# A perceiver kernel on one core: the first feed-forward tile is rounded before the second sequence's gates, and the second output product takes the place of filler matmuls

## The chip, the cores and the metric

One Trainium2 chip, one core. The metric is the device time of one execution in microseconds (us). Engines: PE (TensorE), DVE (VectorE), ACT (ScalarE), POOL (GpSimd) and SP, which here only issues DMAs. TensorE's clock has two levels, 1.2 and 2.4 GHz; the profile gives the granted one as a share of the higher.

## The reference

Two sequences of 256 tokens, 256 features, pass through two layers. What the change touches is the end of the gated mixer and the start of the quantised feed-forward block in layer 0, cut here to its lines:

```python
# gated mixer, end                       # L0_attn
y = _linear(y, fuse_w, fuse_b)
y = gate * y
y = _linear(y, out_w, out_b)
x = residual + y
# feed-forward                           # L0_ffn
h = layernorm(x, ln1_g, ln1_b)
h = bitlinear(h, w1, b1)                 # each row rounded to 8 bits, weights to -1, 0, 1
h = gelu(h)
h = layernorm(h, ln2_g, ln2_b)           # 1024 wide
h = bitlinear(h, w2, b2)
x = x + h
# next layer, cross-attention: scores of layernorm(x) with a context of 4096 rows
```

## The kernel before, in words

The kernel is one program per engine, written out by hand: each engine runs its instructions in the order in which the code lists them, and semaphores (`on[...]`, `wait_ge`, `then_inc`) join the engines. So the order of the lines is the schedule. The 512 tokens are four tiles of 128 rows (0 and 1 are the first sequence, 2 and 3 the second). The first sequence runs ahead: while the mixer of the second sequence is finished, tiles 0 and 1 already go through the feed-forward block.

On the DVE the steps here are `gate(1, m)` (L1505, four chunks of the second sequence, each out of one PSUM bank that `fuse(1, m)` on PE filled), `hidden(0, n)` (L1567: two halves of 512 columns for each tile, PSUM to UH), `hidden_stats` (L1574), `aggregate` (L1429), `ask_root` (L1415, which asks POOL for a power of the variance), `gain` (L1587), `take_power` (waits for POOL), `shift` (L1597), `find_scale` (L1540 to L1546), `quantise_hidden` (L1606 to L1611, which counts up `d_quant2`). After that a tile goes to PE: `turn_hidden(i)` (eight bf16 transposes, L2279), then ACT's `copy_hidden(i)` (L1057), then `project_down(i)` (L2213, eight bf16 matmuls), then DVE's `add_down` (L1614 and statistics) and `centre_for_keys` (L1450), and PE's `turn_tile` (L2292), `queries_tile` and `fold_tile` (L2200, eight fp32 matmul instructions each) and at last the `key_scores` of the next layer (L2448), whose first unit stands behind `turn_hidden(1)` in PE's order.

`project_out(1)` (L2213, 16 instructions) is the mixer's output product of the second sequence. It needs all eight gates; its result is added to X by `add_mixed(2, 4)` (L1510) on DVE. `keep_awake(bank, n)` (L2112) issues n bf16 matmuls of 512 columns whose result nobody reads; they fill PE's waits. ACT's `gelus` (L1048) follow `hidden`. POOL's `power` (L767) computes the roots in the order in which they are asked for.

SP loads the next layer's mask and context (L611); before the first of them it waits for `c_out` at 4, that is the end of `project_out(1)`, and for `d_turned2` at 1, that is `turn_hidden(0)`:

```python
            sp.wait_ge(on["c_out"], 4)
            sp.wait_ge(on["d_turned2"], 1)
```

Of the kernel before, what the change touches and what calls it, by code (L numbers as in the profile page):

```python
# [19 lines left out]
TT = T // P  # L20
# [21 lines left out]
IT = DI // P  # L42
# [107 lines left out]
def build(nc, t):  # L150

    ctx = ExitStack()
    with ctx:
# [3 lines left out]
        def sem(name):  # L157
            return ctx.enter_context(nc.semaphore(name))
# [119 lines left out]
        OUT_BANKS = (7, 0, 3, 4)  # L278
        QUANT_BANK = (1, 3)
        UP_BANKS = ((7, 0, 2, 1), (7, 3, 7, 3))  # L280
        DOWN_BANKS = (5, 6, 3, 7)
        QUERY_BANKS = ((0, 1), (3, 4), (7, 3))
        QC_BANKS = (2, 5, (7, 3))
        CQ_BANK = (5, 6, 7)
# [1 line left out]
        def tile(i):  # L286
            return slice(i * P, (i + 1) * P)

        def batch(b):
            return slice(b * S, (b + 1) * S)  # L290
# [153 lines left out]
        on = {name: sem(name) for name in SIGNALS}  # L444
# [242 lines left out]
        def _(pool):  # L687
# [74 lines left out]
            def power(first, last):  # L762

                powers[0] += 1
                pool.wait_ge(ln_var, powers[0])
                part = SD[:, 4 + first:4 + last]
                nc.gpsimd.tensor_tensor(part, part, NHALF[:, first:last], ALU.pow).then_inc(ln_sd, 1)  # L767

            power(0, 1)
            power(1, 2)  # L770
            power(0, 1)
            power(1, 2)
            power(0, 1)
            power(2, 4)
            power(1, 2)
            power(2, 4)
# [25 lines left out]
        def _(act):  # L802
# [155 lines left out]
            def signal(ins, name):  # L958
                ins.then_inc(on[name], 1)
# [73 lines left out]
            def copy_quantised_tile(i):  # L1033
                act.wait_ge(on["d_turned"], i + 1)
                signal(nc.scalar.activation(HQT[:, :, tile(i)],
                                            psum[:, QUANT_BANK[0], 0:256].bitcast(BF16)
                                            .rearrange("p (c n) -> p c n", c=CT)[:, :, tile(i)], ACT.Copy), "d_turned_copied")
# [6 lines left out]
            def gelus(first, last):  # L1044
                for n in range(first, last):
                    act.wait_ge(on["d_hidden"], n + 1)
                    part = UH[n // 2][:, 0, n % 2 * 512:(n % 2 + 1) * 512]
                    signal(nc.scalar.activation(part, part, ACT.Gelu), "d_gelu")  # L1048
# [6 lines left out]
            def copy_hidden(i):  # L1055
                act.wait_ge(on["d_turned2"], i + 1)
                signal(nc.scalar.activation(QHT[i].rearrange("p k n -> p (k n)"),  # L1057
                                            psum[:, DOWN_BANKS[i], :].bitcast(BF16), ACT.Copy), "d_turned2_copied")

# [6 lines left out]
            def copy_turned_tile(i):  # L1066
                act.wait_ge(ht_psum, CT * (turns[0] + 1))
                nc.scalar.activation(HTE[:, :, tile(i)], psum[:, 7, :].rearrange("p (c n) -> p c n", c=CT)[:, :, tile(i)],
                                     ACT.Copy).then_inc(ht_ready, CT)
                turns[0] += 1  # L1070
# [38 lines left out]
            copy_quantised_tile(0)  # L1109
            gelus(0, 2)  # L1110
            copy_quantised_tile(1)
            gelus(2, 4)
            copy_hidden(0)
            copy_turned_tile(0)
            copy_queries_tile(0)
            copy_folded_tile(0)
# [115 lines left out]
        def _(dve):  # L1232
# [90 lines left out]
            def mark(ins):  # L1323

                ins.then_inc(on["step_v"], 1)
                steps[0] += 1

            def done():

                dve.wait_ge(on["step_v"], steps[0])  # L1330
# [94 lines left out]
            def aggregate(n, first=0, last=TT):  # L1425

                done()
                for i in range(first, last):
                    mark(nc.vector.bn_aggr(MV[:, 2 * i:2 * i + 2], BN[:, 12 * i:12 * i + 6 * n]))  # L1429
                done()  # L1430
# [72 lines left out]
            def gate(b, m):  # L1503
                dve.wait_ge(on["c_fuse"], IT * b + m + 1)
                nc.vector.scalar_tensor_tensor(out=YG[:, m, batch(b)], in0=psum[:, FUSE_BANKS[b][m], 0:S],  # L1505
                                               scalar=col("fuse_b", m), in1=GATE[:, m, batch(b)],
                                               op0=ALU.add, op1=ALU.mult).then_inc(on["c_gated"], 1)
# [56 lines left out]
            def hidden(b, n):  # L1564
                i, at = 2 * b + n // 2, slice(n % 2 * 512, (n % 2 + 1) * 512)
                dve.wait_ge(on["d_up"], 4 * b + n + 1)
                nc.vector.scalar_tensor_tensor(out=UH[i][:, 0, at], in0=psum[:, UP_BANKS[b][n], :],  # L1567
                                               scalar=OSC[:, i:i + 1], in1=row("w1b")[:, at],
                                               op0=ALU.mult, op1=ALU.add).then_inc(on["d_hidden"], 1)

            def hidden_stats(b, n):
                i = 2 * b + n // 2
                dve.wait_ge(on["d_gelu"], 4 * b + n + 1)
                mark(nc.vector.bn_stats(BN[:, 12 * i + n % 2 * 6:12 * i + n % 2 * 6 + 6],  # L1574
                                        UH[i][:, 0, n % 2 * 512:(n % 2 + 1) * 512]))

            def add_down_bias(*tiles):
                done()
                for i in tiles:
                    mark(nc.vector.tensor_tensor(X[:, i, :], X[:, i, :], row("w2b"), ALU.add))  # L1580
# [24 lines left out]
            def quantise_hidden(i):  # L1605
                mark(nc.vector.tensor_scalar(UH[i][:, 0, :], UH[i][:, 0, :], QSC[:, i:i + 1], ROUND,  # L1606
                                             ALU.mult, ALU.add))
                done()
                mark(nc.vector.tensor_scalar(QH[i], UH[i][:, 0, :], ROUND, 127.0, ALU.subtract, ALU.min))
                done()  # L1610
                nc.vector.tensor_scalar(QH[i], QH[i], -128.0, None, ALU.max).then_inc(on["d_quant2"], 1)  # L1611

            def add_down(first, last, ahead):
                add_to_x("d_down", 2, lambda i: nc.vector.scalar_tensor_tensor(  # L1614
                    out=X[:, i, :], in0=psum[:, DOWN_BANKS[i], 0:256], scalar=OSC[:, i:i + 1], in1=X[:, i, :],
                    op0=ALU.mult, op1=ALU.add), first, last, ahead)
                ask_root(first, last)

            def centre_for_keys(*tiles):
                take_power()  # L1620
                for i in tiles:
                    centred(HLE, X, i).then_inc(h_ready, 1)
# [13 lines left out]
            hidden(0, 0)  # L1636
            hidden(0, 1)
            gate(1, 0)
            gate(1, 1)
            hidden_stats(0, 0)  # L1640
            hidden_stats(0, 1)
            aggregate(2, 0, 1)
            ask_root(0, 1)
            gate(1, 2)
            hidden(0, 2)
            hidden(0, 3)
            gain(0)
            gate(1, 3)
            take_power()
            shift(0)  # L1650
            find_scale(0)
            quantise_hidden(0)
            hidden_stats(0, 2)
            hidden_stats(0, 3)
            aggregate(2, 1, 2)
            ask_root(1, 2)
            add_down_bias(0, 1)
            gain(1)
            take_power()
            done()  # L1660
            add_down(0, 1, TT + 2)
            shift(1)
            centre_for_keys(0)
            find_scale(1)
            quantise_hidden(1)
            add_mixed(2, 4, TT + 3)
# [283 lines left out]
        def _(pe):  # L1950
# [158 lines left out]
            def keep_awake(bank, n):  # L2109

                for _ in range(n):
                    nc.tensor.matmul(psum[:, bank, :], IDENTB, IDENTB.unsqueeze(1).broadcast_to((P, 4, P)),  # L2112
                                     start=True, stop=True)
# [140 lines left out]
            def project_out(b):  # L2254
                pe.wait_ge(on["c_gated"], IT * (b + 1))
                for i in (2 * b, 2 * b + 1):
                    linear_rows(psum[:, OUT_BANKS[i], 0:256], tok(YG, i), WOUT, False, "c_out")
# [18 lines left out]
            def turn_hidden(i):  # L2276
                pe.wait_ge(on["d_quant2"], i + 1)
                for k in range(FT):
                    last = nc.tensor.transpose(psum[:, DOWN_BANKS[i], k * 64:(k + 1) * 64].bitcast(BF16),  # L2279
                                               QH[i][:, k * P:(k + 1) * P], IDENTB)  # L2280
                last.then_inc(on["d_turned2"], 1)

            def project_down(i):
                pe.wait_ge(on["d_turned2_copied"], i + 1)
                linear_rows(psum[:, DOWN_BANKS[i], 0:256], [QHT[i][:, k, :] for k in range(FT)], TW2, False, "d_down")

# [40 lines left out]
            def mix():  # L2327
# [83 lines left out]
                project_up(0, 2)  # L2411
                project_up(0, 3)
                fuse(1, 3)
                project_out(1)
                keep_awake(6, 8)

            any_masked = pe.value_load(FLAG, min_val=0, max_val=1)
            with pe.If(any_masked == 0):
# [3 lines left out]
            with pe.Else():  # L2422
                attend(True)
                mix()

            pe.wait_ge(on["d_hidden"], 4)
            turn_hidden(0)
            keep_awake(2, 4)
            project_down(0)
            keep_awake(2, 12)  # L2430
            pe.wait_ge(on["l1w_loaded"], 64)
            turn_tile(HLE, 0, 2 * TT)
            keep_awake(2, 2)
# [456 lines left out]
```

## Time and profile before

| | |
|---|---|
| median of 3 runs | 899.23 us (899.07 to 899.90) |
| the profiled execution, whole | 899.97 us |
| its span | 898.2 us |
| mean granted TensorE clock | 0.998 |
| PE busy | 870.7 us (97%) |
| DVE busy | 606.6 us (68%) |
| ACT busy | 479.8 us (53%) |
| POOL busy | 141.4 us (16%) |

The profiled execution took 1.77 us outside its span and stands 0.74 us above the median. All times of rows are counted from the span's start. Matmul ends are modelled, so a matmul can seem to begin a little before the one ahead of it has ended. In PE's rows an fp32 matmul is two instructions, while the listing of the program's order counts it once.

### The profile page before, as it was taken

The page shows a single profiled execution, that of the slowest core. Times are in us where ns is not written, and L with a number is a line of the kernel's source. Part 1 is how long each engine was busy: PE and PEld are TensorE (multiplying, and loading weights), DVE is VectorE, ACT ScalarE, POOL GpSimd, SP SyncE. Part 2 cuts the span into 40 slices and gives each one's busy share as a digit, 9 for nine tenths or more (in the row PEclk, how much of TensorE's full clock was granted, in tenths as well). Part 3 has the DMA queues.
Part 4 walks back from the last instruction along what each step waited for, and adds up shares of the span by engine and source line. Part 5 has one row for each costly group of instructions (what it writes and reads, how often), then busy time and mean ns, then how long its engine had stood idle before and what let it go on. Part 6 is the DMA issues. An engine that isn't in the chain of part 4 may idle for free.

```text
span 898.2 us, 15321 instructions
## 1 busy us (share of the span) xinstructions
PE 870.7 (97%) x6029; PEld 518.3 (58%) x6031; DVE 606.6 (68%) x1060; ACT 479.8 (53%) x973; POOL 141.4 (16%) x144
## 2 busy tenths in 40 slices
PE   8899999999999999999999999999999999999998
PEld 4556444444556665555545587654884784656745
DVE  6988877778885556888872589977724228379352
ACT  5452666777775566777779852214411310668221
POOL 7353111111000000000000260010100006345100
PEclk9999999999999999999999999999999999999999
DMA  9989564453523112222613440084645705000000
GB/s 353 301 262 221 132 169 113 118 165 112 129 66 90 36 36 72 72 71 72 191 37 136 169 178 1 1 292 138 227 188 186 282 22 167 1 1 1 1 1 24
DMA packets 55083, 108.50 MB, mean 121 GB/s; under 512 B 5409, under 2 KB 38177, under 8 KB 49825
## 3 DMA queue, kind: packets, MB, share of 16 engines
q1 hardware_dynamic: 52832, 103.29, 37.5%
q10 hardware_dynamic: 2176, 4.19, 1.7%
q8 instruction: 50, 0.82, 0.4%
q14 instruction: 25, 0.20, 0.1%
HBM read 93.58 MB, written 13.89 MB: 120 GB/s over the span
## 4 chain that ended last, share of the span: by engine, by line
PE 82%; DVE 11%; ACT 2%; DMA 2%; issue 1%; POOL 1%; SPq 0%; DVEq 0%; ACTq 0%
PE psum L2049 14%; PE psum L2031 13%; PE psum L1998 11%; PE psum L2448 6%; PE psum L2476 6%; PE psum L1961 5%; PE psum L2580 5%; PE psum L1971 4%; DVE arena L1528 3%; PE psum L2213 3%; PE psum L2645 2%; PE psum L2630 2%; PE psum L2200 2%; DVE arena L1281 1%; PE psum L2669 1%
## 5 line engine op out<-in xcount | busy, mean ns | idle before, releaser
L1281 DVE TENSOR_REDUCE arena<-psum 128x1 f32<-128x1024 f32 x256 | 300.9, 1218 | 97.3 <-PE psum L1998 96.8
L849 ACT ACTIVATE arena<-psum 128x512 f32<-128x512 f32 x512 | 263.1, 602 | 67.0 <-PE psum L2031 65.9
L1998 PE MATMUL psum<-arena 120*128 120x512 bf16 x512 | 151.7, 379 | 5.7 <-DVE arena L1281 3.4
L2031 PE MATMUL psum<-arena 120*128 120x256 bf16 x1024 | 154.8, 274 | 1.8 <-ACT arena L849 0.5
L2049 PE MATMUL psum<-arena 128*32 128x256 f32 x2048 | 137.0, 385 | 0.0
L2031 PEld LDWEIGHTS psum<-arena 120*128 120x128 bf16 x1024 | 80.5, 97 | 96.2 <-ACT arena L849 36.7
L2049 PEld LDWEIGHTS psum<-arena 128*32 128x32 f32 x2048 | 53.4, 109 | 74.2 <-ACT arena L849 30.7
L711 POOL TENSOR_TENSOR arena<-arena 128x512 bf16<-128x512 f32 x34 | 41.4, 1219 | 158.3 <-DVE arena L1267 140.4
L1971 PE MATMUL psum<-arena 128*128 128x256 f32 x256 | 63.2, 384 | 0.0
L1998 PEld LDWEIGHTS psum<-arena 120*128 120x128 bf16 x512 | 48.7, 98 | 23.4 <-DVE arena L1281 11.9
L1961 PE MATMUL psum<-arena 128*128 128x512 f32 x128 | 60.9, 603 | 0.0
L2476 PE MATMUL psum<-arena 128*128 128x256 f32 x256 | 57.9, 379 | 0.0
L2448 PE MATMUL psum<-arena 128*128 128x512 f32 x128 | 57.2, 595 | 0.0
L1971 PEld LDWEIGHTS psum<-arena 128*128 128x128 f32 x256 | 47.7, 191 | 13.1 <-issue 5.3
L2476 PEld LDWEIGHTS psum<-arena 128*128 128x128 f32 x256 | 47.5, 190 | 5.8
L735 POOL MEMSET arena<- 128x32 f32 x1 | 0.1, 129 | 288.9 <-PE psum L2049 288.9
L2200 PE MATMUL psum<-arena 128*128 128x256 f32 (+1 forms) x208 | 44.2, 366 | 0.4 <-ACT arena L1075 0.2
L821 ACT ACTIVATE arena<-psum,arena 128x512 bf16<-128x512 f32 x32 | 22.0, 689 | 39.2 <-PE psum L1961 35.6
L832 ACT ACTIVATE arena<-psum 128x512 f32<-128x512 f32 x32 | 19.1, 597 | 44.4 <-PE psum L1971 44.4
L2580 PE MATMUL psum<-arena 128*128 128x512 f32 x96 | 42.8, 596 | 0.0
L2200 PEld LDWEIGHTS psum<-arena 128*128 128x128 f32 x208 | 37.1, 190 | 7.5 <-issue 1.4
L2448 PEld LDWEIGHTS psum<-arena 128*128 128x128 f32 x128 | 23.7, 190 | 25.7 <-issue 24.9
(269 smaller groups left out, 1024.3 us busy)
## 6 DMA issues: line engine op xcount, KB each, us to landing
arena<-mask SPq DMA_DIRECT2D x12, 1024.0 KB, 6.1
kparts<-arena SPq DMA_DIRECT2D x32, 384.0 KB, 3.4
arena<-kparts SPq DMA_DIRECT2D x32, 384.0 KB, 4.6
arena<-ctxT SPq DMA_DIRECT2D x16, 512.0 KB, 5.9
arena<-kparts SPq DMA_DIRECT2D x32, 256.0 KB, 5.1
arena<-ctx SPq DMA_DIRECT2D x2, 4096.0 KB, 17.3
arena<-ctxT ACTq DMA_DIRECT2D x8, 512.0 KB, 8.2
arena<-kparts SPq DMA_DIRECT2D x32, 128.0 KB, 5.5
```

Of the source, the lines that this page charges most:

```text
L711: nc.gpsimd.tensor_tensor(parts[:, 2, :], rest, parts[:, 1, :], ALU.subtract).then_inc(k_low, 1)
L849: nc.scalar.activation(PR[step % 4][:, pair * CH:(pair + 1) * CH], exp_bank(step, pair), ACT.Exp, scale=DH ** -0.5)\
L1281: nc.vector.tensor_reduce(MX[g % 2][:, col:col + 1], unit_banks(n).rearrange("p b n -> p (b n)"), AX.X, ALU.max).then_inc(s_maxed, 1)
L1961: last = nc.tensor.matmul(ring_bank(slot), WK[:, k, f * P:(f + 1) * P], CTX[n % SLOTS][:, k, :], start=(k == 0), stop=(k == CT - 1))
L1971: last = nc.tensor.matmul(ring_bank(slot)[:, v * 256:(v + 1) * 256], CTX[n % SLOTS][:, k, (2 * i + v) * P:(2 * i + v + 1) * P], WV[:, k, : ...
L1998: last = nc.tensor.matmul(out, q, KST[g % 2][0:ROWS, quarter, j, half * CH:(half + 1) * CH], start=True, stop=not masked, skip_group_check ...
L2031: last = nc.tensor.matmul(heads[:, u, :], KST[gg % 2][0:ROWS, kc // 8, j, kc % 8 * P:(kc % 8 + 1) * P], QST[0:ROWS, b, G * g + j, :], star ...
L2049: last = nc.tensor.matmul(PV[32 * j:32 * (j + 1), :], V_flat[:, at:at + 32], PR[step % 4][:, j * S:(j + 1) * S], start=(kc == 0), stop=(kc ...
L2200: last = nc.tensor.matmul(out, weights[:, k, m * P:m * P + width], xs[k], start=(k == 0), stop=(k == n - 1))
L2448: last = nc.tensor.matmul(psum[:, unit % 3, :], QC[:, c, w * P:(w + 1) * P], CTXT[w // 2][:, c, n * 512:(n + 1) * 512], start=(c == 0), st ...
L2476: last = nc.tensor.matmul(psum[:, 6, 0:256], PT1[:, k * P:(k + 1) * P], CTXK[w // 2][:, k, :], start=(k == 0), stop=(k == KC - 1), skip_gr ...
L2580: last = nc.tensor.matmul(out, HTF[:, c, i * P:(i + 1) * P], WQKV[which][:, c, half * HALF:(half + 1) * HALF], start=(c == 0), stop=(c == ...
```

## The change

On DVE everything of tile 0 up to its rounding now stands directly behind its two `hidden` halves and `gate(1, 0)`. The three other gates, tile 1's two `hidden` halves and all of tile 1's steps come behind it. The bias rows and `add_down` of tile 0 stand ahead of tile 1's statistics. On PE `project_out(1)` and the fillers ahead of the branch's end go; `turn_hidden(0)` and `project_down(0)` come first, with 12 and 5 fillers ahead of and between them, and `project_out(1)` stands where 12 fillers stood. Of the four places with 8, 4, 12 fillers (24 in all), 17 are left. Tile 0's transposes and its down product use PSUM bank 0 in place of bank 5. ACT copies tile 0's transposes ahead of tile 1's gelus. On POOL the two requests change places to match.

```diff
-        DOWN_BANKS = (5, 6, 3, 7)
+        DOWN_BANKS = (0, 6, 3, 7)
...
             power(0, 1)
             power(1, 2)
             power(0, 1)
+            power(0, 1)
             power(1, 2)
-            power(0, 1)
...
             copy_quantised_tile(1)
+            copy_hidden(0)
             gelus(2, 4)
-            copy_hidden(0)
...
             gate(1, 0)
-            gate(1, 1)
             hidden_stats(0, 0)
             hidden_stats(0, 1)
             aggregate(2, 0, 1)
             ask_root(0, 1)
-            gate(1, 2)
-            hidden(0, 2)
-            hidden(0, 3)
             gain(0)
-            gate(1, 3)
             take_power()
             shift(0)
             find_scale(0)
             quantise_hidden(0)
+            for m in range(1, IT):
+                gate(1, m)
+            hidden(0, 2)
+            hidden(0, 3)
+            add_down_bias(0, 1)
+            done()
+            add_down(0, 1, TT + 2)
             hidden_stats(0, 2)
             hidden_stats(0, 3)
+            centre_for_keys(0)
             aggregate(2, 1, 2)
             ask_root(1, 2)
-            add_down_bias(0, 1)
             gain(1)
             take_power()
-            done()
-            add_down(0, 1, TT + 2)
             shift(1)
-            centre_for_keys(0)
             find_scale(1)
             quantise_hidden(1)
...
                 fuse(1, 3)
-                project_out(1)
-                keep_awake(6, 8)
...
+            pe.wait_ge(on["d_hidden"], 1)
+            keep_awake(7, 12)
+            turn_hidden(0)
+            keep_awake(7, 5)
+            project_down(0)
             pe.wait_ge(on["d_hidden"], 4)
-            turn_hidden(0)
-            keep_awake(2, 4)
-            project_down(0)
-            keep_awake(2, 12)
+            project_out(1)
             pe.wait_ge(on["l1w_loaded"], 64)
             turn_tile(HLE, 0, 2 * TT)
```

DVE's order behind tile 0's first statistics, as a piece of the difference (the names are those given above; L1505 is a gate, L1567 a hidden half, L1587 the gain, L1597 the shift):

```order
 L1574 BN_STATS arena<-arena 128x6 x2
 L1429 BN_AGGR arena<-arena 128x2
 L1415 TENSOR_SCALAR arena<-arena 128x1
-L1505 SCALAR_TENSOR_TENSOR arena<-psum,arena 128x256
-L1567 SCALAR_TENSOR_TENSOR arena<-psum,arena 128x512 x2
 L1587 SCALAR_TENSOR_TENSOR arena<-arena 128x1024
-L1505 SCALAR_TENSOR_TENSOR arena<-psum,arena 128x256
 L1597 SCALAR_TENSOR_TENSOR arena<-arena 128x1024
 L1540 TENSOR_REDUCE arena<-arena 128x1
```

The request to POOL (L1415) is now followed at once by the gain, and the gain at once by the shift; a gate and two hidden halves stood between the first two and a gate between the others.

The next piece, from the end of tile 0's rounding up to tile 1's shift:

```order
+L1574 BN_STATS arena<-arena 128x6 x2
+L1450 TENSOR_SCALAR arena<-arena 128x256
+L1429 BN_AGGR arena<-arena 128x2
+L1415 TENSOR_SCALAR arena<-arena 128x1
+L1587 SCALAR_TENSOR_TENSOR arena<-arena 128x1024
 L1597 SCALAR_TENSOR_TENSOR arena<-arena 128x1024
-L1450 TENSOR_SCALAR arena<-arena 128x256
 L1540 TENSOR_REDUCE arena<-arena 128x1
```

Tile 1's statistics, its request, gain and shift now stand in a row, behind tile 0's centring (L1450), which stood between tile 1's shift and its scale.

PE before, from `project_out(1)` to the first key scores:

```order
3019 L2213 MATMUL psum<-arena 128x256 x8
3020 L2112 MATMUL psum<-arena 128x512 x8
3021 L2422 UNCONDITIONAL_BRANCH
3022 L2279 MATMUL psum<-arena 128x128 x8
3023 L2112 MATMUL psum<-arena 128x512 x4
3024 L2213 MATMUL psum<-arena 128x256 x8
3025 L2112 MATMUL psum<-arena 128x512 x12
3026 L2292 MATMUL psum<-arena 128x128 x2
3027 L2112 MATMUL psum<-arena 128x512 x2
3030 L2200 MATMUL psum<-arena 128x128 x4
3031 L2279 MATMUL psum<-arena 128x128 x8
3032 L2448 MATMUL psum<-arena 128x512 x2
```

PE now, in the same place (line numbers are one lower than before):

```order
3017 L2419 UNCONDITIONAL_BRANCH
3018 L2111 MATMUL psum<-arena 128x512 x12
3019 L2278 MATMUL psum<-arena 128x128 x8
3020 L2111 MATMUL psum<-arena 128x512 x5
3021 L2212 MATMUL psum<-arena 128x256 x16
3022 L2291 MATMUL psum<-arena 128x128 x2
3023 L2111 MATMUL psum<-arena 128x512 x2
3026 L2199 MATMUL psum<-arena 128x128 x4
3027 L2278 MATMUL psum<-arena 128x128 x8
3028 L2447 MATMUL psum<-arena 128x512 x2
```

The row of 16 is `project_down(0)` with `project_out(1)` behind it; from the turned tile (L2292, now L2291) on the two orders are the same, and the last transposes (L2278) are tile 1's.

## Rows read from the trace of the kernel before

**Rows 1.** The page: the chain that ended last, its shares of the span by engine.

```profile
PE 82%; DVE 11%; ACT 2%; DMA 2%; issue 1%; POOL 1%; SPq 0%; DVEq 0%; ACTq 0%
```

**Rows 2.** Chain that ended last, 587 to 597 us: start us, us, what.

```profile
587.00 1.53 POOL arena L767
...
596.60 5.15 PE psum L2448 x12
```

**Rows 3.** Timeline of DVE: start us, us, engine, line, op, count [idle before <-releaser].

```profile
569.36 1.40 DVE L1567 SCALAR_TENSOR_TENSOR arena<-psum,arena 128x512 f32<-128x512 f32 x2
...
571.43 0.48 DVE L1505 SCALAR_TENSOR_TENSOR arena<-psum,arena 128x256 f32<-128x256 f32 x1 [0.27 <-PE psum L2200]
571.83 1.28 DVE L1574 BATCH_NORM_STATS2 arena<-arena 128x6 f32<-128x512 f32 x2
...
576.88 1.28 DVE L1597 SCALAR_TENSOR_TENSOR arena<-arena 128x1024 f32<-128x1024 f32 x1
...
581.46 0.43 DVE L1611 TENSOR_SCALAR arena<-arena 128x1024 bf16<-128x1024 bf16 x1
...
585.58 0.48 DVE L1614 SCALAR_TENSOR_TENSOR arena<-psum,arena 128x256 f32<-128x256 f32 x1 [0.20 <-DVE arena L1587]
...
586.84 1.27 DVE L1597 SCALAR_TENSOR_TENSOR arena<-arena 128x1024 f32<-128x1024 f32 x1
588.63 0.41 DVE L1450 TENSOR_SCALAR arena<-arena 128x256 f32<-128x256 f32 x1 [0.52 <-POOL arena L767]
...
592.22 0.43 DVE L1611 TENSOR_SCALAR arena<-arena 128x1024 bf16<-128x1024 bf16 x1
...
595.52 0.69 DVE L1676 CUSTOM_DVE_ANT_0 arena<-psum,arena 128x512 f32<-128x512 f32 x1 [1.06 <-PE psum L2448]
```

**Rows 4.** Timeline of POOL: three of its powers.

```profile
563.84 0.73 POOL L767 TENSOR_TENSOR arena<-arena 128x1 f32<-128x1 f32 x1 [1.07 <-DVE arena L1417]
573.62 0.55 POOL L767 TENSOR_TENSOR arena<-arena 128x1 f32<-128x1 f32 x1 [9.05 <-DVE arena L1415]
...
587.00 1.52 POOL L767 TENSOR_TENSOR arena<-arena 128x1 f32<-128x1 f32 x1 [2.76 <-DVE arena L1415]
```

**Rows 5.** Timeline of DVE beside the first of these powers.

```profile
563.68 0.48 DVE L1551 SCALAR_TENSOR_TENSOR arena<-arena 128x256 f32<-128x256 f32 x1
```

**Rows 6.** Timeline of PE, 577 to 594 us.

```profile
577.02 3.72 PE L2213 MATMUL psum<-arena 128*128 128x256 f32 x16 [1.14 <-DVE arena L1505]
580.58 1.89 PE L2112 MATMUL psum<-arena 128*128 128x512 bf16 x8
582.30 0.61 PE L2279 MATMUL psum<-arena 128*128 128x128 bf16 x8
...
584.03 1.05 PE L2213 MATMUL psum<-arena 128*128 128x256 bf16 x8 [0.25 <-ACT arena L1057]
...
589.19 0.41 PE L2292 MATMUL psum<-arena 128*128 128x128 f32 x2 [1.53 <-DVE arena L1450]
...
592.75 0.61 PE L2279 MATMUL psum<-arena 128*128 128x128 bf16 x8
```

**Rows 7.** Timeline of PE, 32 us: the longest wait ahead of a fall of the clock.

```profile
32.59 0.39 PE L2152 MATMUL psum<-arena 128*128 128x8 f32 x2 [2.30 <-DVE arena L1274]
```

**Rows 8.** Busy time by stretch: stretch, us, PE, PEld, DVE, ACT, POOL busy (x), PEclk, DMA share, GB/s.

```profile
33.00:34.00 1.00, 1.00 (x5) 0.90 (x5) 0.93 (x5) 0.00 (x0) 0.33 (x1) 0.90 0.93 213
34.00:35.00 1.00, 1.00 (x3) 0.77 (x3) 1.00 (x1) 0.00 (x0) 0.83 (x1) 0.50 0.92 213
...
37.00:38.00 1.00, 1.00 (x3) 0.22 (x1) 0.73 (x1) 0.00 (x0) 0.64 (x2) 0.89 0.99 221
...
588.00:590.00 2.00, 0.81 (x4) 0.36 (x4) 1.49 (x3) 0.30 (x1) 0.53 (x1) 1.00 0.94 390
```

**Rows 9.** Timeline of the DMA queue of SP: issues of the mask, and their landing.

```profile
583.00 0.82 SPq L611 DMA_DIRECT2D arena<-mask  x2
...
arena<-mask SPq DMA_DIRECT2D x4, 1024.0 KB, 5.0
```

## The prediction

> **What bounds the kernel now.** I read the page's chain first: 82% of the span lies on PE and 11% on DVE [rows 1]. So a microsecond counts where PE waits, or where DVE holds it. Then I read the chain between 557 and 597 us, where the change lies. Up to 593 us it runs mostly over DVE, with one wait for a POOL power [rows 2]; from the first key scores on it stays on PE without a gap (12 instructions in 5.15 us) [rows 2]. The timelines of DVE and PE show why. Two things meet at tile 1's transposes, `turn_hidden(1)` (592.75 us) [rows 6]: PE comes from `fold_tile(0)` just then, and DVE's last rounding instruction of tile 1 ends at 592.22 + 0.43 = 592.65 us [rows 3]. PE is not early: it had been held until 589.19 us by tile 0's centring, with a wait of 1.53 us [rows 6]. The reader should take from this that PE and DVE reach this point together. Whatever happens before it is worth time only if both come earlier, since the key scores stand behind these transposes in PE's order.
>
> **Tile 0 on DVE.** Between `hidden(0, 1)` and the first shift the change takes out three gates and two hidden halves. A gate takes 0.40 us from start to start (571.43 to 571.83), three 1.20, and a wait of 0.27 goes with the first [rows 3]. The two halves are one entry of 1.40 us, 1.32 without the overlap to the next [rows 3]. That is 2.79 us, with small gaps 2.87. Against it stands a new wait. The request to POOL is now followed at once by the gain, an instruction with two SBUF operands of 1024 columns. The trace has that arrangement once, with a shift in place of the gain: the shift began at 586.84 and took 1.27; the power, begun at 587.00, took 1.52 and ended at 588.52, and DVE went on at 588.63 after an idle of 0.52 [rows 3, 4]. With a PSUM operand beside it a power took 0.55 [rows 4]. A third power, begun at 563.84 inside an SBUF pair that ran from 563.68 for 0.48, took 0.73 [rows 4, 5]. In both blocked cases POOL ended 0.41 us after DVE's instruction did. So from gain to shift it is 588.63 - 586.84 = 1.79 us, where 1.31 (1.27 and a drain) would do: the wait costs 0.48. Tile 0's rounding, which ended at 581.46 + 0.43 = 581.89 [rows 3], comes 2.87 - 0.48 = 2.39 earlier, at 579.50.
>
> The Trainium skill says the same of the mechanism (page "SBUF — State Buffer", section "SBUF: two separate sides"): VectorE and GpSimd share a port pair that is locked for a whole instruction, also by a VectorE operation with two SBUF inputs, and the later one waits. The trace agrees, with 1.52 against 0.55 us [rows 4]. [...]
>
> **Tile 1 on DVE, the end that counts.** Up to tile 1's rounding DVE runs the same instructions in both kernels, so only its idle time decides. Before, there were three waits: 0.27 for PE, 0.20 ahead of `add_down`, 0.52 for POOL, 0.99 in all [rows 3]. Now two remain, each a power behind which a gain runs at once: 2 x 0.48 = 0.96. So the rounding of tile 1 ends at 592.65 - 0.99 + 0.96 = 592.62, and with 0.15 from end to release (588.63 + 0.41 to 589.19 [rows 3, 6]) PE begins its transposes at 592.8, where it began at 592.75. **This part is worth 0.0 us**, between -1.0 (no power is held up) and +0.4 (drains between instructions that now stand in another order).
>
> **PE.** `fuse(1, 3)` ended at 577.02 - 1.14 = 575.88 [rows 6]. Twelve fillers at 1.89 / 8 = 0.24 [rows 6] last until 578.7; PE waits for tile 0's rounding until 579.65. From these transposes to the down product it was 584.03 - 582.30 = 1.73 [rows 6], ACT's copy included; so the down product starts at 581.4 and ends at 582.4. `project_out(1)` takes 3.72 [rows 6] and ends at about 586.0. DVE meanwhile: 579.5 and three gates 1.2, two halves 1.4, the bias rows 0.8 (an estimate, two instructions of a gate's width), `add_down` with its statistics 586.84 - 585.58 = 1.26, tile 1's statistics 1.28, centring 0.41 [rows 3], that is 585.8. Both are ready at about 586.0, where it was 589.19. The queries and their folding took until 592.75, 3.56 us, and now end at 589.5. The gain of 3.2 us stops there: **PE waits from 589.5 to 592.8, 3.3 us**, without a filler. The 24 - 17 = 7 fillers that go (1.6 us) lay in waits and are worth nothing on the path.
>
> **The clock.** The longest wait of PE in the trace in the middle of work is 2.30 us, ahead of 32.59 us [rows 7]. 1.2 us after its end the granted clock fell from 2.4 to 1.2 GHz: the five stretches of 1 us from 33 to 38 have 0.90, 0.50, 0.50, 0.50, 0.89 (three of them are [rows 8], the two left out have 0.50 too), in all 1.71 us lost. The wait of 1.53 us behind fillers did not do it: the stretch 588 to 590, with PE busy 0.81 of 2 us, has 1.00 [rows 6, 8]. The new wait of 3.3 us lies above both, and in the 3.5 us before it PE has short waits as well. I expect the fall. What it costs: PE pays only while it works. If the fall comes as long after the last matmul as it did there (30.3 to 33.8 us), it comes at 593.0 and all of the 1.7 us is paid by the key scores, which nothing hides. If it comes inside the wait, a part goes by unused; halfway in, 0.85. Nearest to the row is the full price, but the moment need not repeat; I take 1.5.
>
> **Transfers.** The masks wait for both `project_out(1)` and `turn_hidden(0)`. They were issued at 583.00 [rows 9]; now `project_out(1)` is the later, so 586.0. With 5.0 us to landing [rows 9] they are there at 591, and the first mask is read at 595.52 [rows 3]: nothing, with 4.5 us in hand. Bank 0 was last read by `hidden(0, 1)`, at 570.7: nothing. ACT is idle where its copy moves to: nothing. If ACT still had tile 1's gelus ahead, the copy would come 1.3 us later; they now stand behind it and wait for DVE anyway.
>
> **Sum.** 899.97 (own time of the profiled execution) + 0.0 + 1.5 = 901.5; against the median, which is 0.74 lower, 899.23 + 1.5 = **900.7 us**.
>
> **Rivals.** (a) The clock stays at 2.4 GHz: 899.2. For it speaks that all waits below 2.3 us went by without a fall; against it the 3.3 us. (b) The powers are not held up, by shorter locks or since POOL gets in first: DVE is 0.96 earlier, 898.3 with a steady clock, 899.8 with a fall. Against it speak two held-up powers out of two. (c) The gain of 3.2 us on PE is kept: 896.0. It would need tile 1's rounding at 589.5, and DVE has no 3 us of idle to give up (0.99). (d) Slower: the low clock is not left after one stretch like that of rows 8. While PE stands partly idle in the stretch after the fall, it may stay down for a second one, 2 x 1.7 = 3.4 us: 902.6. It decides if the fall comes well inside the wait, since then the next stretch holds waiting as well. (e) The change is not what it says on PE, if the fillers ahead of the transposes held up tile 0: they end at 578.7, 0.9 us early, so no.
>
> **Chances.** A measurement tells 0.2% (1.8 us, 897.4 and 901.0) from no change. Forecast, one fall: 0.68, of which about 0.22 comes out above 901.0 by a full price and drains of 0.1 to 0.4. (a) 0.13. (b) 0.06. (c) 0.03. (d) 0.10. So faster 0.04, same 0.63, slower 0.33. The range takes in (a) and most of (b) with a fall, and most of (d): 898.9 to 902.3.
>
> **What would show it.** PE waits over 3 us ahead of the second L2278 and DVE's L1611 ends within 0.4 us of 592.65; both powers of this place take 1.5 us. Tile 0's turned tile (L2291) starts at 586. A stretch with a granted clock of 0.5 lies between 591 and 597 us; key scores of 1.72 us last twice as long in it. Wrong would be: a clock of 1.00 throughout, L1611 a microsecond early, or a wait of the first mask for its DMA.

## The result, and the profile after

The changed kernel takes 901.15 us in the median of 22 runs (899.92 to 903.34); the kernel before, run beside it, 899.83 us in 22 runs. The ratio of the two is 1.0018 with a 95% interval of 1.0012 to 1.0024: slower by 1.3 us, an amount just under the 0.2% that the prediction took as the border of "same". The forecast was +1.5 us and 900.7 us.

DVE first. The timeline of DVE in the changed kernel: start us, us, engine, line, op, forms, count [idle before <-releaser]. This execution reached `hidden(0, 0)` at 570.02 where the one before had 569.36 [rows 3], so 0.66 us are to be taken off to compare.

```profile
570.02 1.40 DVE L1567 SCALAR_TENSOR_TENSOR arena<-psum,arena 128x512 f32<-128x512 f32 x2
...
573.36 1.27 DVE L1587 SCALAR_TENSOR_TENSOR arena<-arena 128x1024 f32<-128x1024 f32 x1
575.15 1.28 DVE L1597 SCALAR_TENSOR_TENSOR arena<-arena 128x1024 f32<-128x1024 f32 x1 [0.51 <-POOL arena L767]
...
579.73 0.43 DVE L1611 TENSOR_SCALAR arena<-arena 128x1024 bf16<-128x1024 bf16 x1
...
583.36 0.48 DVE L1614 SCALAR_TENSOR_TENSOR arena<-psum,arena 128x256 f32<-128x256 f32 x1
...
586.44 1.28 DVE L1587 SCALAR_TENSOR_TENSOR arena<-arena 128x1024 f32<-128x1024 f32 x1
588.23 1.28 DVE L1597 SCALAR_TENSOR_TENSOR arena<-arena 128x1024 f32<-128x1024 f32 x1 [0.51 <-POOL arena L767]
...
592.82 0.43 DVE L1611 TENSOR_SCALAR arena<-arena 128x1024 bf16<-128x1024 bf16 x1
...
598.00 0.69 DVE L1675 CUSTOM_DVE_ANT_0 arena<-psum,arena 128x512 f32<-128x512 f32 x1 [2.95 <-PE psum L2447]
```

Tile 0's rounding (first L1611) ends at 580.16, less the offset 579.50, where it ended at 581.89: 2.4 us earlier. Tile 1's (second L1611) ends at 593.25, less the offset 592.59, where it ended at 592.65: the same. The waits of 0.27, 0.20 and 0.52 us [rows 3] have gone, and two of 0.51 us for POOL have come: idle time on DVE is about what it was.

POOL in the changed kernel, its timeline at the same place:

```profile
573.52 1.52 POOL L767 TENSOR_TENSOR arena<-arena 128x1 f32<-128x1 f32 x1 [8.29 <-DVE arena L1415]
584.78 0.55 POOL L767 TENSOR_TENSOR arena<-arena 128x1 f32<-128x1 f32 x1 [9.74 <-DVE arena L1415]
586.60 1.52 POOL L767 TENSOR_TENSOR arena<-arena 128x1 f32<-128x1 f32 x1 [1.27 <-DVE arena L1415]
```

The first and third power run beside a gain, the second beside statistics, which read one SBUF operand. Of three equal operations two take 1.52 us and one 0.55.

PE in the changed kernel, its timeline from the down product on:

```profile
580.22 0.62 PE L2278 MATMUL psum<-arena 128*128 128x128 bf16 x8 [1.09 <-DVE arena L1611]
...
581.95 4.50 PE L2212 MATMUL psum<-arena 128*128 128x256 bf16 x24
586.36 0.41 PE L2291 MATMUL psum<-arena 128*128 128x128 f32 x2
...
588.92 1.16 PE L2199 MATMUL psum<-arena 128*128 128x128 f32 x8 [0.24 <-ACT arena L1075]
593.30 1.03 PE L2278 MATMUL psum<-arena 128*128 128x128 bf16 x8 [3.22 <-DVE arena L1611]
594.12 3.73 PE L2447 MATMUL psum<-arena 128*128 128x512 f32 x4
```

Tile 0's turned tile starts at 586.36 (585.70 less the offset), where it started at 589.19 [rows 6]: 3.5 us earlier. All of it ends up in one wait of 3.22 us ahead of tile 1's transposes. The unit of key scores behind it then takes 3.73 us. The busy time in stretches of 1 us shows why (stretch, us, PE, PEld, DVE, ACT, POOL busy (x), PEclk, DMA share, GB/s):

```profile
591.00:592.00 1.00, 0.00 (x0) 0.00 (x0) 0.96 (x3) 0.00 (x0) 0.00 (x0) 1.00 0.99 418
592.00:593.00 1.00, 0.00 (x0) 0.00 (x0) 0.93 (x3) 0.00 (x0) 0.00 (x0) 0.50 0.97 410
...
597.00:598.00 1.00, 1.00 (x4) 0.48 (x3) 0.00 (x0) 0.00 (x0) 0.00 (x0) 0.50 1.13 356
598.00:599.00 1.00, 1.00 (x7) 0.86 (x7) 0.70 (x2) 0.00 (x0) 0.00 (x0) 0.58 1.06 344
```

The granted clock fell from 2.4 to 1.2 GHz at 592.0, 1.3 us before PE had work again, and stayed there to 598.8. The 12 instructions of key scores that follow began at 596.60 [rows 2], 27.24 us after `hidden(0, 0)`; now the chain of work that ended last (start us, us, what) has them at 599.60, 29.58 us after it, so this execution paid 2.3 us:

```profile
593.30 1.03 PE psum L2278 x8
594.33 3.52 PE psum L2447 x4
597.85 0.65 PE psum L2306 x4
598.50 1.11 PE psum L2212 x8
599.60 5.15 PE psum L2447 x12
```

The other executions have no trace, but each has a mean granted clock: 15 of 22 have 0.996, four less, one 0.998 and two 1.00. Those two took 899.92 and 900.00 us. In the 35 executions of the kernel before that ran with the first experiments, 24 have 0.998, ten 1.00 and one 0.996.
The masks were issued later, as expected, and no instruction waited for them; the first masked score waited for PE (2.95 us above). The DMA queue of SP:

```profile
586.49 0.82 SPq L611 DMA_DIRECT2D arena<-mask  x2
```

### The profile page after: what moved, and what is told of

Its sections match the earlier page's. It is cut to its first block, busy times and chain, and to the rows that moved or that the text cites. A ratio compares the mean times of both kernels' runs of the same rounds, so it can differ in the third digit from the quotient of the medians.

```text
span 901.2 us, 15308 instructions
## 1 busy us (share of the span) xinstructions
PE 870.7 (97%) x6024; PEld 519.2 (58%) x6024; DVE 607.0 (67%) x1060; ACT 480.0 (53%) x973; POOL 142.3 (16%) x144
## 4 chain that ended last, share of the span: by engine, by line
PE 82%; DVE 12%; ACT 2%; issue 2%; DMA 1%; POOL 1%; SPq 0%; DVEq 0%; ACTq 0%
PE psum L2048 14%; PE psum L2030 13%; PE psum L1997 12%; PE psum L2447 6%; PE psum L2475 6%; PE psum L1970 5%; PE psum L2579 5%; PE psum L1960 5%; DVE arena L1528 3%; PE psum L2212 3%; DVE arena L1281 2%; PE psum L2644 2%; PE psum L2629 2%; PE psum L2668 1%; PE psum L2459 1%
## 5 line engine op out<-in xcount | busy, mean ns | idle before, releaser
L1970 PEld LDWEIGHTS psum<-arena 128*128 128x128 f32 x256 | 48.0, 192 | 13.4 <-issue 5.9
L2475 PEld LDWEIGHTS psum<-arena 128*128 128x128 f32 x256 | 47.5, 190 | 5.8
L2199 PEld LDWEIGHTS psum<-arena 128*128 128x128 f32 x208 | 37.1, 190 | 7.5 <-issue 1.4
L1675 DVE CUSTOM_DVE_ANT_0 arena<-psum,arena 128x512 f32<-128x512 f32 x32 | 22.0, 691 | 25.6 <-PE psum L2447 23.2
```

Of the source, the lines that this page charges most:

```text
L1970: last = nc.tensor.matmul(ring_bank(slot)[:, v * 256:(v + 1) * 256], CTX[n % SLOTS][:, k, (2 * i + v) * P:(2 * i + v + 1) * P], WV[:, k, : ...
L2199: last = nc.tensor.matmul(out, weights[:, k, m * P:m * P + width], xs[k], start=(k == 0), stop=(k == n - 1))
L2475: last = nc.tensor.matmul(psum[:, 6, 0:256], PT1[:, k * P:(k + 1) * P], CTXK[w // 2][:, k, :], start=(k == 0), stop=(k == KC - 1), skip_gr ...
```

## The experiments

All ratios are to the kernel before, run beside each group. The first question was whether the clock is all of the loss.

**Fillers in the wait.**

```diff
             fold_tile(0)
+            keep_awake(6, 13)
             turn_hidden(1)
```

> The changed kernel with 13 fillers (2.8 us) between fold_tile(0) and turn_hidden(1), where PE waited 3.22 us. DVE and everything else are as changed. Theory A (the loss is the fall of TensorE's clock in that wait): the granted clock stays at 1.00 from 586 to 600 us, tile 1's rounding still ends when it did after the change, the key scores take 1.72 us a unit from the first on, and the time goes back to that of the kernel before, 899.8 us, 1.3 us under the changed kernel. Theory B (the loss is something else that came with the change, a later end of DVE, the later masks or the order of the output product): the clock is back but the time stays at 901.1 us.

Measured: 899.75 us against 899.89, ratio 0.9995 (0.9986 to 1.0004). The executions' mean clock is 0.998 in nine and 1.00 in two of 11. PE's timeline of this kernel:

```profile
589.52 2.97 PE L2111 MATMUL psum<-arena 128*128 128x512 bf16 x13
592.89 0.62 PE L2278 MATMUL psum<-arena 128*128 128x128 bf16 x8 [0.41 <-DVE arena L1611]
593.35 1.94 PE L2448 MATMUL psum<-arena 128*128 128x512 f32 x4
```

Theory A holds. Thirteen matmuls that compute nothing take the loss away, and what the rest of the change costs or gains lies within the interval, -1.3 to +0.4 us.

**The reverse, on the kernel before.**

```diff
             project_down(0)
-            keep_awake(2, 12)
```

> The kernel before without the 12 fillers behind project_down(0); nothing else differs. PE then waits 4.2 us in place of 1.5 for tile 0's centring at 589 us. Theory A (a wait of that length drops the clock and the drop costs time): the granted clock falls to 0.5 between 587 and 592 us, the queries and the folding, and perhaps the first key scores, run at half speed, and the time rises by 0.5 to 1.7 us to 900.3 to 901.5 us, with DVE's rounding of tile 1 still at 592.65 us. Theory B (fillers and the clock do not matter here): 899.8 us, clock 1.00.

Measured: 901.36 us against 899.89, ratio 1.0016 (1.0008 to 1.0025), and a mean clock of 0.996 or less in ten of 11 executions. PE's timeline, and one stretch of busy time (columns as above):

```profile
589.81 0.66 PE L2292 MATMUL psum<-arena 128*128 128x128 f32 x2 [4.12 <-DVE arena L1450]
...
595.11 0.61 PE L2279 MATMUL psum<-arena 128*128 128x128 bf16 x8
```

```profile
588.00:590.00 2.00, 0.19 (x1) 0.23 (x2) 1.48 (x3) 0.00 (x0) 1.14 (x1) 0.50 1.00 422
```

With the wait at 4.12 us the clock is at 1.2 GHz before PE goes on. The queries and their folding, 3.56 us before, take 595.11 - 589.81 = 5.30 us, so tile 1's transposes come 1.7 us later, although DVE's rounding is where it was (the offset of this execution, 0.62 us, taken off). In this trace the clock is low once only, in one piece from 588.0 to 594.8 us, and the mean is 0.996: the same mean as two separate falls would give. Theory A again: a loss of the same size, with nothing of the change in the kernel.

**Half the fillers.** As the first edit, with `keep_awake(6, 6)`.

> The changed kernel with 6 fillers in place of 13 ahead of turn_hidden(1), so that 1.8 us of PE's wait are left. Theory A (it is the length of the wait that drops the clock; in the kernel before 1.5 us of wait did not): the mean clock is that of the kernel before (0.998) in nearly all executions, 899.8 us. Theory B (any wait here drops it, since PE was only partly busy ahead of it): a mean clock of 0.996 in most executions, 900.5 to 901 us.

Measured: 900.61 us against 900.16, ratio 1.0007 (0.9998 to 1.0016); the mean clock is 0.996 in seven of 11 executions, 0.998 in two, 1.00 in two. The execution with the profile is one of the last kind, so its trace shows the wait but no fall:

```profile
588.96 1.46 PE L2111 MATMUL psum<-arena 128*128 128x512 bf16 x6
592.34 0.62 PE L2278 MATMUL psum<-arena 128*128 128x128 bf16 x8 [1.92 <-DVE arena L1611]
```

By the executions' mean clock theory A fails here: with a wait of about 1.9 us at this place most executions have a low stretch more than usual, though with 1.53 us the kernel before did not (34 of 35). The time, 0.45 us above the kernel before, does not decide it, since its interval takes in no change. The two waits differ in more than 0.4 us. The one of 1.53 stood behind 12 fillers in a row; this one behind six, ahead of which PE had waited 0.24 us for a copy of ACT. Which of the two matters, the length or the work ahead, was not separated.

**Real work in the wait.** The first unit of key scores goes ahead of tile 1's transposes.

```diff
             fold_tile(0)
-            turn_hidden(1)
             pe.wait_ge(on["e_qc_copied"], 1)
...
             key_scores(0, 0)
+            turn_hidden(1)
             bias_tile(0)
             project_down(1)
```

> The changed kernel with the first unit of key scores, key_scores(0, 0), ahead of turn_hidden(1) on PE, so that real work lies in the wait. Theory A (PE's 3.2 us were gained and stop at tile 1's transposes): the unit runs at full clock from about 590.6 to 592.4 us, the wait for tile 1's rounding falls to about 0.6 us, the clock stays at 1.00, and the end comes 1.7 us earlier than with a steady clock alone: 898.1 us, 3 us under the changed kernel. Theory B (DVE sets the stretch after it too, since the masked scores wait behind tile 1's rounding and the adding of the mixer): the clock is steady but nothing else is gained, 899.8 us.

Measured: 899.02 us against 899.89, ratio 0.9993 (0.9984 to 1.0001). PE's timeline, the last row being tile 1's turned tile behind the next key scores:

```profile
589.53 1.99 PE L2445 MATMUL psum<-arena 128*128 128x512 f32 x4 [0.47 <-ACT arena L1080]
592.27 0.62 PE L2278 MATMUL psum<-arena 128*128 128x128 bf16 x8 [0.76 <-DVE arena L1611]
...
594.01 1.05 PE L2212 MATMUL psum<-arena 128*128 128x256 bf16 x8 [0.72 <-ACT arena L1057]
...
600.05 0.38 PE L2291 MATMUL psum<-arena 128*128 128x128 f32 x2
```

The same row in the kernel before:

```profile
601.59 0.38 PE L2292 MATMUL psum<-arena 128*128 128x128 f32 x2
```

The gain came out between the theories: the median is 0.9 us under the kernel before in place of 1.7, but by its interval the time alone does not tell it from no change. The trace does. Up to tile 1's turned tile the same work has been done in both; it starts 601.59 - 569.36 = 32.23 us after `hidden(0, 0)` before, and 600.05 - 569.00 = 31.05 us after it here, 1.2 us less. The trace also names what is missing: the moved unit had covered ACT's copy of tile 1 (L1057), and without it PE waits 0.72 us ahead of the down product. My expectation had left that cover out. The next run puts another unit there.

```diff
             key_scores(0, 0)
             turn_hidden(1)
+            key_scores(0, 1)
             bias_tile(0)
             project_down(1)
-            key_scores(0, 1)
             key_scores(0, 2)
```

> As the run with key_scores(0, 0) ahead of turn_hidden(1), but with key_scores(0, 1) moved between turn_hidden(1) and project_down(1). There PE had waited 0.72 us for ACT's copy of tile 1, which the moved unit had covered. Theory A (1.7 us of work moved, 0.7 given back by that uncovered copy): the wait of 0.72 us goes, the masked scores on DVE follow their unit as before, and the time falls by 0.5 to 0.7 us more, to 898.4 us. Theory B (DVE's masked scores, released later than their units, bound this stretch): the wait comes back ahead of key_scores(0, 3), which needs the first bank, and the time stays at 899.0 us.

Measured: 897.90 us against 900.16, ratio 0.9975 (0.9966 to 0.9984).

```profile
593.72 0.62 PE L2278 MATMUL psum<-arena 128*128 128x128 bf16 x8 [0.76 <-DVE arena L1611]
594.18 1.94 PE L2445 MATMUL psum<-arena 128*128 128x512 f32 x4
...
596.32 1.03 PE L2212 MATMUL psum<-arena 128*128 128x256 bf16 x8
...
600.62 0.38 PE L2291 MATMUL psum<-arena 128*128 128x128 f32 x2
```

The wait of 0.72 us is gone, and the kernel is 2.3 us faster than the one before; the changed one was 1.3 us slower than it, so the two lie 3.6 us apart. Theory A on the mechanism. Its step of 0.5 to 0.7 us was too small: the medians of the two runs differ by 1.1 us (0.9 and 2.3 under the kernel before beside each), and tile 1's turned tile starts 600.62 - 570.45 = 30.17 us after `hidden(0, 0)`, 0.9 us less than in the last run.

**The same on the kernel before.** Both moves of scores, nothing of the change.

> The kernel before with the same order on PE (key_scores(0, 0) ahead of turn_hidden(1), key_scores(0, 1) behind it), and nothing of the change. There PE reaches this point as tile 1's rounding ends, so there is no wait to fill. Theory A: nothing is gained, 899.8 us (within 0.3). Theory B (the scores gain by being early, whatever PE waited for): 898.4 us, as in the changed kernel. The difference to the run on the changed kernel is what the change's 3.2 us on PE are worth once work lies in them.

Measured: 900.37 us against 900.16, ratio 1.0006 (0.9997 to 1.0015), no gain. PE gets to its scores at 594.20 and goes from them to tile 1's transposes without a wait:

```profile
594.20 1.98 PE L2446 MATMUL psum<-arena 128*128 128x512 f32 x4 [0.47 <-ACT arena L1080]
596.02 0.61 PE L2279 MATMUL psum<-arena 128*128 128x128 bf16 x8
```

Ahead of the scores PE now waits 0.47 us for ACT's copy of the queries, which `turn_hidden(1)` had covered. So the early scores gain nothing by themselves, and the change alone, with the clock kept up by fillers, gains nothing that the times can tell; the two together gain 2.3 us. It is the change that puts PE 3 us ahead, and the scores that use it.

**The waits for POOL.** Two gates between tile 0's request and its gain, tile 0's centring between tile 1's.

```diff
             ask_root(0, 1)
+            gate(1, 1)
+            gate(1, 2)
             gain(0)
...
-            for m in range(1, IT):
-                gate(1, m)
+            gate(1, 3)
...
-            centre_for_keys(0)
             aggregate(2, 1, 2)
             ask_root(1, 2)
+            centre_for_keys(0)
             gain(1)
```

> The changed kernel with two gates between tile 0's request to POOL and its gain, and with tile 0's centring between tile 1's request and its gain; same instructions. Theory A (POOL's power is held up by the gain, since both want SBUF and the gain begins 0.16 us before it): both powers take 0.55 to 0.7 us in place of 1.52, the two DVE waits of 0.51 us go (the second may leave 0.1 to 0.3, since centring covers only 0.33 us), and tile 1's rounding ends 0.7 to 1.0 us earlier. PE's wait shrinks from 3.2 to 2.4 us and the clock still falls in most executions: 900.2 to 900.5 us. Theory B (a power takes 1.5 us whenever DVE is busy): both still take 1.5 us, DVE still waits, 901.1 us.

Measured: 900.93 us against 899.89, ratio 1.0010 (1.0002 to 1.0019), which doesn't differ from the changed kernel's 1.0018 (1.0012 to 1.0024). The mean clock is 0.996 in eight of 12 executions; the profiled one (899.40 us) has no fall here, ahead of tile 1's transposes, where PE waited 2.44 us. POOL's timeline, then two rows of DVE's:

```profile
572.61 0.55 POOL L767 TENSOR_TENSOR arena<-arena 128x1 f32<-128x1 f32 x1 [8.29 <-DVE arena L1415]
...
585.80 0.65 POOL L767 TENSOR_TENSOR arena<-arena 128x1 f32<-128x1 f32 x1 [1.08 <-DVE arena L1415]
```

```profile
573.07 0.48 DVE L1505 SCALAR_TENSOR_TENSOR arena<-psum,arena 128x256 f32<-128x256 f32 x1 [0.15 <-PE psum L2200]
...
582.75 0.48 DVE L1614 SCALAR_TENSOR_TENSOR arena<-psum,arena 128x256 f32<-128x256 f32 x1 [0.57 <-PE psum L2213]
...
591.87 0.43 DVE L1611 TENSOR_SCALAR arena<-arena 128x1024 bf16<-128x1024 bf16 x1
```

On the mechanism theory A is right: the powers take 0.55 and 0.65 us in place of 1.52, and both waits of 0.51 us are gone. On the gain it failed. From the first power's start to tile 1's last rounding step it is 591.87 - 572.61 = 19.26 us, where the changed kernel has 592.82 - 573.52 = 19.30. The second gate waited for PE, tile 0 reached PE later for the two gates ahead of it, and DVE then stood 0.57 us for tile 0's down product. That is 0.72 us of new waits for 1.02 us of old ones; the rest went into the gaps between instructions that no longer follow each other. One wait had been traded for another. With this order on DVE and the best order of scores:

> The same order on PE, and on DVE the two gates and the centring between request and gain. Theory A (DVE's two POOL waits then set the last wait of PE, 0.76 us ahead of turn_hidden(1)): both powers take 0.55 to 0.65 us, tile 1's rounding ends 0.9 us earlier, PE's wait goes, and the time falls by another 0.7 us to 897.7 us, 0.24% under the kernel before and 3.4 us under the changed one. Theory B (the wait moves to DVE's masked scores): as the run without the split, 898.4 us.

Measured: 897.83 us against 900.16, ratio 0.9975 (0.9964 to 0.9985), the same as without the split. The figure lies near theory A's 897.7, but by luck: the run without the split had turned out at 897.90 in place of the assumed 898.4. On the gain theory A failed once more, for the reason just given. PE's last wait of 0.76 us is gone only since PE comes 0.75 us later, through tile 0. With one gate in place of two (`gate(1, 2)` back behind the rounding):

> The changed kernel with the best order of the scores (key_scores(0, 0) ahead of turn_hidden(1), key_scores(0, 1) behind it), and between tile 0's request and its gain only one gate, not two; tile 0's centring stands between tile 1's request and gain as before. With two gates the second waited 0.15 us for PE, and tile 0 reached PE so late that DVE then waited 0.57 us for its down product, so that tile 1's rounding came no earlier. Theory A (the two waits for POOL, 1.02 us, are real cost if nothing else takes their place): tile 1's rounding ends 19.3 - 0.75 = 18.5 us after tile 0's first request to POOL starts there, PE's wait of 0.76 us ahead of turn_hidden(1) shrinks to 0.1, and the time falls from 897.9 to 897.2 us. Theory B (some other wait always takes their place): 19.2 us and 897.9 us.

Measured: 897.23 us against 899.94, ratio 0.9970 (0.9957 to 0.9982). DVE's and PE's timelines:

```profile
582.51 0.48 DVE L1614 SCALAR_TENSOR_TENSOR arena<-psum,arena 128x256 f32<-128x256 f32 x1 [0.18 <-PE psum L2213]
...
591.63 0.43 DVE L1611 TENSOR_SCALAR arena<-arena 128x1024 bf16<-128x1024 bf16 x1
```

```profile
590.14 1.98 PE L2446 MATMUL psum<-arena 128*128 128x512 f32 x4 [0.47 <-ACT arena L1080]
592.11 0.62 PE L2279 MATMUL psum<-arena 128*128 128x128 bf16 x8
...
599.01 0.38 PE L2292 MATMUL psum<-arena 128*128 128x128 f32 x2
```

The first power begins at 573.01 in this execution, so it is 18.62 us to the last rounding step, 0.68 less than in the changed kernel, and PE passes to tile 1's transposes without a wait. Tile 1's turned tile starts 599.01 - 569.51 = 29.50 us after `hidden(0, 0)`, 0.7 us less than the 30.17 without the split. The time agrees (897.23 and 897.90 us in the medians, 2.7 and 2.3 us under the kernel before beside each), but with only six executions the intervals overlap; the trace, not the time, carries this step. It is the fastest kernel of the study, 0.3% under the one before.

**One gate, with fillers.**

> The same DVE order with 13 fillers in the wait and the scores where the changed kernel has them. The clock is steady, so this prices the two waits for POOL by themselves. The fillers end about 0.4 us ahead of tile 1's rounding, so PE can take only that much: Theory A: 899.8 - 0.4 = 899.4 us, with no wait of PE ahead of turn_hidden(1). Theory B: as with the fillers alone, 899.8 us, PE still waits 0.4 us.

Measured: 899.00 us against 899.94, ratio 0.9990 (0.9981 to 1.0000). PE's wait of 0.41 us ahead of the transposes is gone here too, and tile 1's turned tile starts 31.41 us after `hidden(0, 0)` in place of 31.88 with the fillers alone: theory A. The point value lies 0.4 us below its forecast; against the fillers alone (0.9995) the intervals overlap.

## Why the prediction was right or wrong

**Bound.** Right: a gain up to tile 1's transposes is worth nothing unless both PE and DVE come earlier. The fillers showed it: with PE 3.5 us ahead at tile 0's turned tile and a steady clock the time is that of the kernel before, within its interval.

**Tile 0 on DVE.** Right: 2.39 us were forecast, 579.50 against 579.50 measured with the offset taken off. The wait for POOL was forecast at 0.48 us of cost and showed as 0.51 of idle. What the Trainium skill says (page "SBUF — State Buffer", section "SBUF: two separate sides"), that an operation of VectorE with two SBUF inputs locks GpSimd out until it ends, agrees with the powers that began behind such an operation (in the traces before and after 1.52 us three times, and 0.73 beside the shorter one, against 0.55), and the split made the waiting go. That page gives about 115 ns behind VectorE's end as the time until which GpSimd stays blocked, measured on another operation, and not as the time at which its operation has ended; here POOL's record ends at 575.04, 0.41 us after the gain's (573.36 + 1.27), and it is this end that DVE waits for. How much of the 0.41 is the power's own work no run shows. The other direction of what the prediction took from the page, that the later one waits, the runs with gates do not bear out (last section).

**Tile 1 on DVE.** Right: 592.62 was forecast, 592.59 measured. Counting idle time on one engine between two fixed points, and not the moved instructions one by one, made this easy.

**PE.** Right in kind and nearly in size: a wait of 3.3 us forecast, 3.22 measured. The turned tile was forecast at 586.0 and came at 585.7, since the forecast added whole durations where neighbours overlap by some 0.1 us each (on PE the two products took 4.41 us from start to turned tile, not 1.0 + 3.72).

**The clock.** Right that it would fall and that the time would rise for it. The term was 1.5 us. The medians differ by 1.3 us, and the two executions that kept a clock of 1.00 throughout lie about 1.2 us below the median. The working behind the term is not borne out by the one trace there is. The prediction let the fall come 3.5 us after PE's last matmul, at the end of the wait, with one low stretch behind it. In the profiled execution it came at 592.0, 1.9 us after PE's last matmul had ended (588.92 + 1.16 = 590.08) and inside the wait, and the clock stayed at 1.2 GHz for 6.8 us, twice the stretch of [rows 8], at a price of 2.3 us. That is rival (d), with the condition that the prediction gave for it; this execution is the second slowest of the 22. That the median execution paid for a single low stretch is inferred from its mean clock of 0.996; no trace shows where that stretch lies. So the closeness of 1.5 and 1.3 is in part luck: the price runs from nothing (two executions) to 2.3 us and more. The bound below was wrong as well. Rival (a) let waits "below 2.3 us" pass without a fall, on the row of 1.53 us; with 1.92 us the mean clock shows a fall in most executions of the run with six fillers.

**The time.** 900.7 us was forecast, 901.15 measured, inside the range. The miss of 0.45 us is the sum of two: the start was 0.6 us too low (the kernel before had 899.23 us in three runs and 899.83 in 22), and the added term 0.2 too high. The difference was forecast at 1.5 and is 1.3 us, which is "same" by the border of 0.2%, as the likeliest case had it, and yet clear of zero by its interval.

**Transfers, bank, ACT.** Right: the masks were issued at 586.49 and not waited for; PE's transposes of tile 0 waited for DVE's rounding and not for bank 0; ACT had been idle when its copy of tile 0 came.

## What to carry to other kernels

When a change makes one of two engines earlier at the place where they meet, look at what the freed engine does there. Here an empty wait of 3.2 us on TensorE was worse than no head start at all, since in most executions the clock fell in it. The head start was worth something only once independent work stood in the wait, and then what that work had covered at its old place had to be covered anew. Between a request to GpSimd and the wait for it, put VectorE instructions that read at most one operand from SBUF, but only such as are ready and hold up nothing else: here one gate of 0.40 us, with the centring at the other request, gained 0.7 us, and two gates gained nothing.

## What had not been expected of the hardware

The same wait does not always bring a fall. In the profiled execution of the kernel before the clock fell at 33.8 us, behind PE's wait of 2.30 us [rows 7, 8]. In that of the changed kernel, whose program is the same up to there, PE had the same wait of 2.30 us and the clock stayed at 1.00; it fell at 39.0, behind a further wait of 2.13 us (PE's timeline, then a stretch of busy time):

```profile
38.73 1.60 PE L1997 MATMUL psum<-arena 120*128 120x512 bf16 x4 [2.13 <-issue]
```

```profile
39.00:40.00 1.00, 1.00 (x4) 0.50 (x3) 0.49 (x1) 0.00 (x0) 0.04 (x1) 0.52 1.08 381
```

So one trace cannot tell what a given wait costs; the share of many executions in which the clock falls can. And a power that starts 0.16 us ahead of a gain (585.80 and 585.96 in the run with two gates) did not hold the gain up: POOL took 0.65 in place of 0.55 us, and the gain its 1.28 us.
